# Second attention normalised as its value products leave PSUM, closing keys spread from the PSUM bank, squares and last sum on DVE

## The reference, cut to what matters

```
x = x + cross(layernorm(x), ctx)   # 16 heads of 64, keys and values from 257 context rows of 192
x = x + attn(layernorm(x))         # 16 heads of 16, inside one sequence of 32 tokens
x = x + ffn(layernorm(x))          # sigmoid(r) * (relu(k)**2 @ Wv), r and k from x mixed with its shift

# attn, the block that the change touches most:
q, k, v = split(x_n @ W_qkv + b_qkv)
scores = q @ k.T * 16 ** -0.5;  e = exp(scores - max(scores))
ctx = (e / maximum(sum(e), 1e-12)) @ v          # per head
out = ctx @ W_proj + b_proj
```

## Time and profile before

| | |
|---|---|
| median of 3 runs | 835.1 us (832.51 to 836.73) |
| the profiled execution | 835.4 us, of which its span 832.8 |
| granted TensorE clock, mean | 0.995 |
| PE busy | 801.4 us, 96% |
| DVE busy | 599.3 us, 72% |
| ACT busy | 604.6 us, 73% |
| POOL busy | 417.0 us, 50% |

### The profile page before, as it was taken

The page is one execution under the profiler, slowest core; times in us unless marked ns, Lnnn a source line. Parts: engine busy times, 40 slices in busy tenths (PEclk is TensorE's granted clock), DMA queues, the critical chain, the costliest instruction groups (busy, mean ns, idle before and its releaser), DMA issues.

```text
span 832.8 us, 20494 instructions
## 1 busy us (share of the span) xinstructions
PE 801.4 (96%) x7497; PEld 665.5 (80%) x7497; DVE 599.3 (72%) x1813; ACT 604.6 (73%) x1439; POOL 417.0 (50%) x664
## 2 busy tenths in 40 slices
PE   9999899998999999998999989999999999999976
PEld 8988688885889778896788868887688977978755
DVE  4865857787587966879577886778668794688376
ACT  3998857887678965789568976789667895778333
POOL 1356445762456624665347534566245672487311
PEclk9999999999999999999999999999999999999999
DMA  8411210111101201012101111011010110100000
GB/s 234 140 32 44 55 26 15 39 27 39 27 15 39 65 1 39 2 40 64 27 15 27 26 52 27 14 39 48 18 27 14 39 52 14 28 14 1 27 2 13
DMA packets 49522, 30.51 MB, mean 37 GB/s; under 512 B 22928, under 2 KB 48336, under 8 KB 49424
## 3 DMA queue, kind: packets, MB, share of 16 engines
q1 hardware_dynamic: 48528, 29.12, 12.9%
q10 hardware_dynamic: 896, 0.10, 0.1%
HBM read 26.85 MB, written 2.10 MB: 35 GB/s over the span
## 4 chain that ended last, share of the span: by engine, by line
PE 79%; DVE 16%; issue 3%; ACT 1%; DMA 0%; POOL 0%; POOLq 0%; ACTq 0%
PE score L807 18%; PE probT L818 6%; PE pre L657 6%; PE post L895 6%; DVE qk_t L1356 5%; DVE qk_l L1352 3%; PE aux L746 3%; PE post L904 3%; PE ac_main L835 3%; PE ac_tail L837 3%; PE ac_main L836 3%; PE ac_tail L841 3%; PE ac_main L840 3%; PE post L875 2%; PE post L881 2%
## 5 line engine op out<-in xcount | busy, mean ns | idle before, releaser
L431 POOL TENSOR_TENSOR prT_l<-prT,prT_h 128x512 fp32r<-128x512 f32 x128 | 165.3, 1292 | 187.0 <-ACT prT_h L1128 186.5
L565 POOL TENSOR_SCALAR pr<-pr,rsum,poison 128x257 f32<-128x257 f32 x256 | 149.4, 594 | 134.8 <-DVE rsum L1380 134.8
L1109 ACT ACTIVATE pr<-sm,nmx 128x257 f32<-128x257 f32 x256 | 129.5, 507 | 61.2 <-DVE nmx L1374 58.1
L1374 DVE CUSTOM_DVE_ANT_0 sm<-score,mbias 128x257 f32<-128x257 f32 x256 | 106.8, 420 | 75.3 <-PE score L807 60.6
L807 PE MATMUL score<-cT_h,qk_h 128*128 128x258 f32 x256 | 89.7, 350 | 7.3 <-DVE qk_t L1356 6.0
L1128 ACT ACTIVATE prT_h<-prT 128x512 fp32r<-128x512 f32 x128 | 80.5, 630 | 20.3 <-PE ac_tail L841 19.1
L1117 ACT ACTIVATE prT<-probT 128x512 f32<-128x512 f32 x128 | 75.6, 591 | 6.7 <-PE probT L818 4.7
L818 PE MATMUL probT<-ident,pr 128*128 128x128 f32 x512 | 79.3, 277 | 0.0
L807 PE MATMUL score<-cT_h,qk_t 128*128 128x258 f32 x256 | 72.8, 284 | 0.0
L807 PE MATMUL score<-cT_h,qk_l 128*128 128x258 f32 x256 | 72.5, 283 | 0.0
L807 PE MATMUL score<-cT_l,qk_h 128*128 128x258 f32 x256 | 72.5, 283 | 0.0
(11 more groups left out here) (319 smaller groups left out, 2170.2 us busy)
## 6 DMA issues: line engine op xcount, KB each, us to landing
cx_in<-in_ctx_dram SPq DMA_DIRECT2D x64, 192.0 KB, 2.5
cx_in<-in_ctx_dram SPq DMA_DIRECT2D x64, 64.0 KB, 2.3
xn<-in_x_dram SPq DMA_DIRECT2D x8, 256.0 KB, 2.9
xb<-in_x_dram SPq DMA_DIRECT2D x8, 256.0 KB, 3.0
out_dram<-yo SPq DMA_DIRECT2D x7, 256.0 KB, 2.2
wq<-in_L_xattn_Wq_dram SPq DMA_DIRECT2D x2, 512.0 KB, 6.0
wo<-in_L_xattn_Wo_dram SPq DMA_DIRECT2D x1, 1024.0 KB, 8.2
wqkv<-in_L_attn_W_qkv_dram SPq DMA_DIRECT2D x1, 768.0 KB, 8.9
```

The source lines that it names most:

```text
L431: eng.tensor_tensor(prT_l[:, :, cut], prT[:, :, cut], prT_h[:, :, cut], ALU.subtract).then_inc(prob_lower, 1)
L565: last = pool.tensor_scalar(p, p, rsum[:, j % 2, t:t + 1], poison[:, 0:1], ALU.mult, ALU.mult)
L1109: act.activation(pr[j % 2][:, t, :], sm[:, t % 2, :], ACT.Exp, bias=nmx[:, j % 2, t:t + 1], scale=-1.0, accum_out=ssum[:, j % 2, t:t + 1]) ...
L1374: dve.tensor_tensor_reduce(sm[:, t % 2, :], score[t % 2][:, 0:NK], mbias[:], DH ** -0.5, BIG, ALU.add, ALU.min, nmx[:, j % 2, t:t + 1]).th ...
```

## The change

1. The product by the reciprocals is taken off the probabilities. W0, W1 are gone; PT0 and PT1 wait for the exponential alone. PV leaves PSUM through DVE, which multiplies by the reciprocals of the sums, in place of an ACT copy.
2. In the close KM.a on DVE reads KT.a's PSUM bank itself, adds the bias and multiplies by the mask in one operation. ACT's copy of KT.a is gone, and the bank is free once DVE is done.
3. In the close KA.0, KA.1 and YO.1 are on DVE. YO.0 stays on POOL.
4. All orders of the middle groups and of the last are written anew, with one fill fewer (16). In the close OT1.0, OT0.1 and OT1.1 come before WO.0 and WO.1, and the stages C of the two halves alternate.

```diff
 # PE, last group and close
-... S3:7 P1:6 FV P0:7 AC:6 OT0.0 P1:7 LT.1 OT1.0 AC:7 WO.0 OT0.1 OT1.1 Z0 WO.1 T2.0 QT.0 KT.0 Z1 T2.1 QT.1
-KT.1 Z2 SC.0 Z3 Z4 Z5 VR.0 Z6 SC.1 Z7 VR.1 PT.0 PV.0 Z8 T4.0 PT.1 PJ.0 PV.1 Z9 T4.1 PJ.1 Z10 T3.0 Z11 Z12 Z13 Z14
-T3.1 FR.0 FK.0 FR.1 Z15 FK.1 Z16 FV.0 FV.1
+... FK AC:6 FV P1:7 LT.1 OT0.0 AC:7 OT1.0 OT0.1 OT1.1 WO.0 WO.1 Z0 T2.0 QT.0 KT.0 T2.1 QT.1 KT.1
+SC.0 Z1 Z2 Z3 VR.0 PT.0 SC.1 PV.0 Z4 VR.1 T4.0 PT.1 PV.1 PJ.0 T4.1 PJ.1 Z5 Z6 Z7 Z8 Z9 T3.0 Z10 Z11 T3.1 Z12 FR.0
+FK.0 FR.1 FK.1 Z13 Z14 FV.0 Z15 FV.1
 # DVE, close
-... KM.0 KM.1 SC.0 VR.0 SM.0 SC.1 VR.1 SM.1 PJ.0 C0.0 ... C9.0 PJ.1 C0.1 ... C9.1 M1.0 M1.1 FR.0 FR.1 SG.0 SG.1 FV.0 FV.1
+... KM.0 KM.1 SC.0 VR.0 SM.0 SC.1 PV.0 VR.1 SM.1 PV.1 PJ.0 C0.0 C1.0 C2.0 C3.0 C4.0 C5.0
+PJ.1 C6.0 C0.1 C7.0 C1.1 C2.1 C8.0 C3.1 C9.0 C4.1 C5.1 C6.1 C7.1 C8.1 C9.1 M1.0 M1.1 FR.0 KA.0 SG.0 FR.1 KA.1 FV.0
+SG.1 FV.1 YO.1
 # middle groups, around SC1 on PE; around SC1 and around FV on DVE; the end on PE
-SC0 CT:5 P1:2 S0:4 S1:4 Q1 AC:2 S2:4 SC1 ... FV K0 K2 P0:7 AC:6 K4 K6 P1:7 LT K8 AC:7 CT:0 K10
+SC0 CT:5 P0:3 S2:4 S3:4 AC:2 P1:3 SC1 ... FV K0 K2 AC:6 P0:7 K4 P1:7 K6 LT K8 AC:7 CT:0 K10
-SC0 KM2 AC:1 S0:4 KM3 CT:5 SM0 R1:3 S1:4 S2:4 SC1 ... SG1 R1:7 FV CL:7 AC:5 K0 K1
+SC0 R0:4 S2:4 KM2 S3:4 KM3 SM0 CT:5 SC1 ... SG1 CL:7 FV R0:7 AC:5 K0 R1:7 K1
 # ACT, middle groups: PT1's copy behind AC:2
-AC:2 E1 P0:3 PT0 U0:3 Q2 S3:4 PT1
+E1 CU:4 PT0 AC:2 PT1
 # PE
-                    pe.wait_ge(p2_ready, 2 * g + w + 1)
+                    pe.wait_ge(sexp_done, 2 * g + w + 1)
 # DVE
+                    dve.tensor_tensor(mine, parts, rs2[:, own].unsqueeze(3).broadcast_to([P, own.stop - own.start, SH, SD]),
+                                      ALU.mult).then_inc(post_copied["VectorE"], 1)
...
-                    dve.wait_ge(*copied(name.replace("KM", "KT"), g))
+                    dve.wait_ge(post_full, issued(name.replace("KM", "KT"), g))
...
+                        last = dve.scalar_tensor_tensor(out=kM_half[a][:, c], in0=keys[:, c * P:(c + 1) * P].unsqueeze(1).broadcast_to([P, 8, P]),
+                                                        scalar=bcol[:, 2 + c:3 + c], in1=headm[:].unsqueeze(2).broadcast_to([P, 8, P]),
+                                                        op0=ALU.add, op1=ALU.mult)
```

More of the change, by code:

```diff
@@ L86 @@
 ACT_ORDER = (
[4 rows of a table removed]
-    "P1:6 CU:7 AC:5 U1:6 K0 K1 K2 K3 P0:7 AC:6 K4 K5 U0:7 K6 P1:7 K7 U1:7 K8 K9 CT:0 K10 K11 AC:7").split()
-ACT_LAST = (
[5 rows of a table removed]
-    "T3.0 M0.0 T3.1 M0.1 FK.0 EZ.0 FK.1 EZ.1").split()
[4 rows of a table added]
+    "U0:6 LV1 U1:6 K0 K1 K2 K3 AC:6 P0:7 K4 K5 U0:7 P1:7 K6 U1:7 K7 K8 K9 CT:0 K10 K11 AC:7").split()
+ACT_LAST = (
[5 rows of a table added]
+    "FK.0 EZ.0 FK.1 EZ.1").split()
 DVE_FIRST = (
@@ L105 @@
 DVE_ORDER = (
[4 rows of a table removed]
-    "S2:7 S3:7 CL:6 R0:7 SG1 R1:7 FV CL:7 AC:5 K0 K1 K2 K3 AC:6 K4 K5 LT K6 K7 K8 K9 CT:0 K10 K11 AC:7").split()
-DVE_LAST = (
[6 rows of a table removed]
-    "C8.0 C9.0 PJ.1 C0.1 C1.1 C2.1 C3.1 C4.1 C5.1 C6.1 C7.1 C8.1 C9.1 M1.0 M1.1 FR.0 FR.1 SG.0 SG.1 FV.0 FV.1").split()
[4 rows of a table added]
+    "CL:6 R1:6 SG0 S3:7 SG1 CL:7 FV R0:7 AC:5 K0 R1:7 K1 K2 K3 AC:6 K4 K5 LT K6 K7 K8 K9 CT:0 K10 K11 AC:7").split()
+DVE_LAST = (
[7 rows of a table added]
+    "SG.1 FV.1 YO.1").split()
 POOL_FIRST = (
@@ L133 @@
 N_FIRST_QK = 2 * len(FIRST_QK)
-ACT_POST = ("OT0", "OT1", "T2", "QT", "KT", "PT0", "PT1", "PV", "T4", "T3", "FK")
-DVE_POST = ("WO0", "WO1", "VR", "SC0", "SC1", "PJ", "FR", "FV")
+ACT_POST = ("OT0", "OT1", "T2", "QT", "KT", "PT0", "PT1", "T4", "T3", "FK")
+DVE_POST = ("WO0", "WO1", "VR", "SC0", "SC1", "PV", "PJ", "FR", "FV")
 POST_NAMES = ACT_POST + DVE_POST
@@ L147 @@
 OF_GROUP = ("LX", "LT")
-FILL = tuple(f"Z{n}" for n in range(17))
+FILL = tuple(f"Z{n}" for n in range(16))
 TP = TOK // 2
@@ L388, in copied @@
                 return post_copied["VectorE"], DVE_COPIED[name, g]
+            if name in ("KT.0", "KT.1"):
+                return post_copied["VectorE"], DVE_COPIED[name.replace("KT", "KM"), g]
             return post_copied["ScalarE"], ACT_COPIED[name, g]
@@ L907, in post_job @@
                     w = int(name[-1])
-                    pe.wait_ge(kM_ready, 4 * g + 2 * w + 2)
+                    if a is None:
+                        pe.wait_ge(kM_ready, 4 * g + 2 * w + 2)
+                    else:
+                        pe.wait_ge(*copied(f"KT.{a}", g))
                     keys = kM if a is None else kM_half[a]
@@ L963, in post_job @@
                 elif base == "FV":
-                    pe.wait_ge(ka_ready, g + (a or 0) + 1)
+                    if a is None:
+                        pe.wait_ge(ka_ready, g + 1)
+                    else:
+                        pe.wait_ge(ka_last, a + 1)
                     mine = ka if a is None else ka_half[a]
@@ L1192, in post_job @@
                 elif base == "KT":
-                    keys = kT2 if a is None else kT2_last
                     for k in range(2):
-                        last = act.activation(keys[:, k, part], bank[:, k * n_tok:(k + 1) * n_tok], ACT.Identity, bias=bcol[:, 2 + k:3 + k])
+                        last = act.activation(kT2[:, k, part], bank[:, k * n_tok:(k + 1) * n_tok], ACT.Identity, bias=bcol[:, 2 + k:3 + k])
                 elif base in ("PT0", "PT1"):
@@ L1198, in post_job @@
                     last = act.activation(probs.rearrange("p c q -> p (c q)"), bank[:], ACT.Copy)
[L1199 to L1202, removed]
-                        last = act.activation(cv_last[:, a, :], bank[:, 0:DM], ACT.Copy)
                 elif base == "T4":
@@ L1421, in post_job @@
                 elif base == "KM":
-                    dve.wait_ge(*copied(name.replace("KM", "KT"), g))
+                    dve.wait_ge(post_full, issued(name.replace("KM", "KT"), g))
+                    keys = post_bank(name.replace("KM", "KT"), g)
                     for c in range(2):
-                        dve.tensor_tensor(kM_half[a][:, c], kT2_last[:, c, a * P:(a + 1) * P].unsqueeze(1).broadcast_to([P, 8, P]),
-                                          headm[:].unsqueeze(2).broadcast_to([P, 8, P]), ALU.mult).then_inc(kM_ready, 1)
+                        last = dve.scalar_tensor_tensor(out=kM_half[a][:, c], in0=keys[:, c * P:(c + 1) * P].unsqueeze(1).broadcast_to([P, 8, P]),
+                                                        scalar=bcol[:, 2 + c:3 + c], in1=headm[:].unsqueeze(2).broadcast_to([P, 8, P]),
+                                                        op0=ALU.add, op1=ALU.mult)
+                    last.then_inc(post_copied["VectorE"], 1)
                 elif base[:2] == "KM":
@@ L1460, in post_job @@
                     last.then_inc(post_copied["VectorE"], 1)
+                elif base == "PV":
+                    dve.wait_ge(post_full, issued(name, g))
+                    dve.wait_ge(srecip_done, 2 * g + rows_of[-1] + 1)
+                    mine = (cv if a is None else cv_last)[:, own].rearrange("p a (h d) -> p a h d", d=SD)
+                    parts = bank[:, 0:width].rearrange("p (a h d) -> p a h d", h=SH, d=SD)
+                    dve.tensor_tensor(mine, parts, rs2[:, own].unsqueeze(3).broadcast_to([P, own.stop - own.start, SH, SD]),
+                                      ALU.mult).then_inc(post_copied["VectorE"], 1)
                 elif base == "PJ":
@@ L1502, in post_job @@
                         dve.tensor_tensor(gate, bank[:, 0:width], gate, ALU.mult).then_inc(post_copied["VectorE"], 1)
+                    elif base == "KA":
+                        dve.wait_ge(*copied(name.replace("KA", "FK"), g))
+                        dve.tensor_tensor(ka_half[a], kr_half[a], kr_half[a], ALU.mult).then_inc(ka_last, 1)
+                    elif base == "YO":
+                        dve.wait_ge(*copied(name.replace("YO", "FV"), g))
+                        dve.wait_ge(stored, 16 * g)
+                        dve.tensor_tensor(yo[:, a, :], gate, x2[:, a, :], ALU.add).then_inc(y_last, 1)
             def key_weights(n):
```

36 lines of the change are left out of this document (15 added, 21 removed), and 55 rows, old and new, of tables (ACT_LAST, ACT_ORDER, DVE_LAST, DVE_ORDER).

## The result

The changed kernel takes **832.6 us** (median of 20 runs, 831.8 to 833.3) where the kernel before took 834.4 (20 runs in the same series, 832.5 to 836.7): a ratio of 0.9983, 95% interval 0.9975 to 0.9990. That is 1.8 us less, inside the 0.5% that count as no change, where 4.6 less had been forecast. The profiled execution took 833.2 us with a span of 830.5.

A forecast was written before the change was run, and what follows sets the result against it. PE, busy 96% of the span, was taken as the bound, with idle time mostly in the close. Middle groups 0, last group -0.5 and close -4.1 summed to -4.6, taking 835.1 to 830.5 us; range 826.5 to 835.0.

The forecast's parts named there:

- Part 1: Six middle groups: the new order leaves PE's jobs, neighbour costs and key-product waits alike; 0 us, bounds -2.4 to +3.0.
- R4: Rival, middle groups: PE stands at SC1 for KM3; at 1.5 us a group lost, 839.5 us; chance 0.12.
- Part 2: Second attention inside the groups: in the last group PT0's wait for POOL goes; -0.5 us, bounds -1.6 to +1.0.
- (a): Start of the close: OT products ahead of both W_o halves leave no place for a fill and idle time; -0.9 us.
- (b): Close, KM.1 read from the PSUM bank: DVE waits for PE alone, not ACT's copy; -0.5 us, spread taken as 2.4.
- (c): Close, KM.1 to PJ.1: PT.1 waits for the exponential alone, DVE's queue is next; -3.9 us, 1.3 of it clock.
- (d): Close, third norm, PJ.1 to T3.1: alternating halves put half of the first's stages between the second's; +1.0 us.
- (e): End of the close: squares on DVE +0.8, one DVE sum replacing two on POOL -0.6; net +0.2 us.
- R1: Rival, close: the clock falls again, so (c) gives 1.3 less; taken as 831.9 us; chance 0.12.
- R2: Rival, close: DVE takes on POOL's and ACT's work, (c) without the clock is 1.0, not 2.6; 832.1 us; chance 0.10.
- R3: Rival, middle groups: CL:7 ahead of FV and freer copies shorten key products by 0.4 us each; 828.1 us; chance 0.16.

## Why the prediction was wrong, and where it was right

The forecast was 4.6 us less, and 1.8 less were measured. The close and the last group gained 1.6 us more than forecast, and the six middle groups lost 3.6 us where the forecast put 0. That the whole came out faster at all is owed to the close alone. The prediction's own mark, the middle moving by more than 0.5 us a group, was passed with 0.6. Point by point, in the profiled executions:

- **Part 1, the step that failed: "the value taken is 0 for the six groups".** I had priced the new order at 0.0 to 0.5 us a group; it costs 0.6 in each, +3.6 in all, beyond even the bound of +3.0. The part on neighbours was right: PE's jobs cost the same in both orders, and the key products also kept their time. I had named two tight places; the first, SC1 waiting for KM3, is not there (no wait of L913 for kM), and the second, PT1 behind ACT's copies, is not what ends the wait. What I had not followed is the one between them: PT0 writes the bank that SC1's subtraction empties, and the new order of DVE puts SM0 and CT:5 ahead of SC1. The hand sum of DVE's work ended with KM3 and took all durations from undisturbed rows; 1.07 of the floor's 1.25 us are a collision with POOL, which the order newly brings about. The six groups together take 590.15 us before and 593.72 after. Without the collision they take 589.92 (floor left out), 589.78 (floor as a reduction) and 590.94 (old order with the edit, of which 0.56 is the wait for a transfer). The reduction keeps the new order, the instruction's place and its waits, so the whole 3.6 us are due to the collision; the queue by itself costs nothing measurable.
- **R4** gave the sign and the sum of a middle that gets longer, and its mark (over 99 us a group) was reached to the tenth (98.96 to 99.04). Its place and its releaser were wrong (the chain does run over both KM, but as part of DVE's queue ahead of SC1's subtraction), and at 0.6 us a group it stayed below the 0.8 at which it would have eaten the gain.
- A reading of the earlier trace rows in the prediction is off and changes nothing: the other five middle groups take 98.07 to 98.53 us, not 98.35 to 98.52.
- **Part 2**, last group: -0.5 forecast, -0.85 measured.
- **(a)** -0.9 forecast, -0.79 measured (the second W_o half ends after 99.66 us in place of 101.30, of which 0.85 belong to part 2).
- **(b)** -0.5 forecast; KM.1 starts 0.65 earlier behind W_o and takes 2.48 us for 2.36, together -0.53. My 2.4 for the spread from PSUM was 0.08 short. The Trainium skill, VectorE: DVE Perf Modes, Rules for kernel authors, names the copy only for many operations and leaves the other way open; that it would have kept the copy for two was the prediction's reading. By the runs here dropping it is right (with the copy, and ACT's order for it, 1.0 us later).
- **(c)**, the largest term: -3.9 forecast, -4.59 measured (11.90 us from KM.1's end to PJ.1, for 16.49). The fills in the kernel before put 1.73 of it on the clock, where I had 1.3; the remaining 2.86 compare with 2.6. How they divide between POOL's product and the new order of PE and DVE no run separates.
- **(d)** +1.0 forecast, +0.20 measured: I charged the first half's stages in full to the second, and they mostly fill its hand-overs.
- **(e)** +0.2 forecast, +0.24 measured, but for another reason: with the squares back on POOL it stays, and with the norms in sequence it goes.
- R1 fell (the clock reads 1.00 until PE's last products), R2 and R3 too.

The close with part 2 was forecast at -4.6 and gave -6.24; most of that difference is (c), 0.7, and (d), 0.8. The start of the second group is 0.37 us late in this profile; in the profiles of kernels with the same first group it lies anywhere between 99.2 and 100.2 us, so I give it no cause. What remains open is the 0.25 us of one group of the old order with the edit.

## What to carry to other kernels

Where a hand-written order is changed, look not only at which jobs stand in the queue but at which operations of DVE and POOL will newly overlap: an instruction of 0.17 us became one of 1.25. In the profile such a collision shows in the least and most of a line's records, not in its mean; look for lines with a wide spread whose most sits on the chain. One that sits elsewhere costs nothing: the kernel before has such collisions too (below). A change of form can remove it without touching the order. And for every bank with two users in a row, follow the reader that empties it, on its own engine's queue.

## What the runs showed of the hardware

An operation of DVE and one of POOL can exclude each other, and it goes by their forms. DVE's one-operand TENSOR_SCALAR and its TENSOR_TENSOR on 128x16 numbers in SBUF took 1.25 us beside POOL's TENSOR_TENSOR, ending 0.03 us after it; TENSOR_REDUCE took 0.17 in the same place. With the floor left out, RECIPROCAL on the same numbers took its usual 0.25 there, and the TENSOR_TENSOR behind it, with one operand in PSUM (CT:5's lower part), 0.63. In the other direction POOL's two products of the weights at 543.85 took 3.18 us together, beside DVE's two KM products of 1.25 and 1.23:

```profile
L568 POOL TENSOR_SCALAR pr<-pr,rsum,poison x256: 550/558/1603, 31.1 to 773.4; 128x257 f32<-128x257 f32 x128
```

Their median is 0.56, their most 1.60, and the DVE instructions were not slowed (1.25 and 1.23, the median of the line being 1.22). By the Trainium skill, SBUF — State Buffer, SBUF: two separate sides, DVE in a two-port mode or with two inputs in SBUF shares a pair of ports with GpSimd, and the one that starts first holds it for its whole instruction. The three forms of the floor agree with that (1.25, 1.25 and 0.17). In the other direction the order of the starts is not borne out by the records: POOL's product is recorded from 543.85, DVE's from 543.93, and it was POOL that waited.

The kernel before has such collisions as well, in each of its six middle groups. DVE's TENSOR_SCALAR on 128x2 numbers (a norm stage, L1305) took 0.69 us where its median is 0.17, and ended 0.04 us after POOL's TENSOR_TENSOR; POOL's CAST of 128x2 (L549) took 1.20 for 0.19 beside a KM product of DVE.

```profile
506.51 1.04 POOL L559 TENSOR_TENSOR lv<-lvc,keep 128x512 f32<-128x512 f32 x1
```

```profile
506.90 0.69 DVE L1305 TENSOR_SCALAR lw<-lw 128x2 int32<-128x2 int32 x1
```

The chain of waits touches neither of them there. So the new order did not bring collisions into a kernel that had none; it brought one onto the chain.

Of the clock: in the kernel before it read its lower level from 808.06 to 814.89 us, after PE had stood 1.25 us ahead of PT.0 and during the 0.79 us ahead of PV.0. In the changed close PE stood 1.12, 0.75 and 0.81 us ahead of PT.0, PV.1 and PJ.1 and the clock stayed at its upper level. With the keys copied by ACT it stayed up after a stand of 1.40 us ahead of SC.0 and one of 0.66 ahead of PT.0. In the kernel before, with 1.04 us of fills in the first stand and 0.52 in the second, it did not fall either, although PE then stood 1.22 us ahead of PT.1. So the length of the longest stand does not decide it by itself; what does, these runs do not show.
